# Six tiles' decay chain instead of two ahead of a scan, and the order of two copies on ScalarE

## What is computed

```python
# soft mixture: each token's row is a weighted mean of 8 x 128 processed slots
out = einsum('bnd,bsn->bsd', processed.reshape(b, e*t, d), softmax(logits.reshape(b, s, e*t)))
x = x + gb * out
# layer 1: modulated layer norm, then a second layer norm, then the projection W_in
h = layernorm(x) * (1 + ca) + sa
normed = layer_norm(h, gamma, beta)
dt = softplus(normed @ W_in[:, -8:] + b_in + dt_bias)      # one value a token and head
decay = exp(dt * A)                                        # 8 heads
h_t = decay_t * h_{t-1} + (dt_t * xs_t) B_t ; y_t = C_t h_t
```

## Time and profile before

| | |
|---|---|
| time, median of 3 runs | 1759.81 us (1759.13 to 1760.4) |
| the profiled execution | 1759.81 us, its span 1758.1 us |
| PE busy | 1642.9 us, 93% of the span |
| DVE busy | 1209.1 us, 69% |
| ACT busy | 732.0 us, 42% |
| POOL busy | 544.9 us, 31% |
| granted TensorE clock, mean | 0.98 |
| the combining loop of b = 1, with its tail | 845.3 to 931.2 us |

### The profile page before, as it was taken

How to read it: one execution, slowest core, us unless ns; L and a number is a source line. 1 busy time by engine, 2 the same in 40 slices (tenths; PEclk the granted TensorE clock), 3 DMA queues, 4 the chain that set the end, 5 groups by cost and what they waited for, 6 DMA issues and landing times. The chain is left out here.

```text
span 1758.1 us, 25512 instructions
## 1 busy us (share of the span) xinstructions
PE 1642.9 (93%) x9248; PEld 1383.2 (79%) x9248; DVE 1209.1 (69%) x2662; ACT 732.0 (42%) x1443; POOL 544.9 (31%) x446
## 2 busy tenths in 40 slices
PE   6999989989999999979987999999989999999996
PEld 4788878888867888856876888888768787888895
DVE  6877678764435655636686899999967845666663
ACT  3333333343324234424525666666621224444442
POOL 2100020000000003222252666666600023777764
PEclk9999999999999999989987999999999999999998
DMA  6000000010010000020116122232141123656553
GB/s 221 4 1 1 1 1 1 1 49 1 1 48 1 1 13 13 29 95 26 52 33 209 61 76 76 76 87 81 63 145 60 60 60 119 171 134 171 132 128 37
DMA packets 80248, 111.55 MB, mean 63 GB/s; under 512 B 15982, under 2 KB 60154, under 8 KB 79868
## 3 DMA queue, kind: packets, MB, share of 16 engines
q1 hardware_dynamic: 66172, 91.43, 16.1%
q0 software_dynamic: 12288, 17.31, 5.5%
q10 hardware_dynamic: 1664, 1.18, 0.2%
HBM read 81.59 MB, written 27.68 MB: 62 GB/s over the span
## 5 line engine op out<-in xcount | busy, mean ns | idle before, releaser
L2915 POOL DMA_INDIRECT out<-k_eo,idx x64 | 117.3, 1832 | 75.4 <-DVE k_eo L3007 60.7
L1816 POOL DMA_INDIRECT k_xe<-rows_dram,idx x64 | 82.5, 1289 | 178.8 <-DVE idx L2848 140.7
L1665 PE MATMUL d_pO<-d_sp,d_raw 128*128 128x257 f32 x512 | 116.6, 385 | 2.8 <-ACT d_raw L1460 2.7
L1665 PEld LDWEIGHTS d_pO<-d_sp,d_raw 128*128 128x128 f32 x512 | 96.9, 192 | 18.1 <-ACT d_raw L1460 3.5
L537 ACT ACTIVATE b_p<-b_pS,b_nmax 128x2048 f32<-128x2048 f32 (+14 forms) x32 | 40.6, 1270 | 141.2 <-DVE b_nmax L678 141.2
L61 PE MATMUL b_pO<-b_vh,b_ph 128*128 128x256 f32 x302 | 88.0, 291 | 4.4 <-DVE b_pl L660 4.3
L62 PE MATMUL b_pO<-b_vh,b_pl 128*128 128x256 f32 x302 | 85.7, 284 | 0.0
L63 PE MATMUL b_pO<-b_vl,b_ph 128*128 128x256 f32 x302 | 85.5, 283 | 0.0
L333 POOL TENSOR_TENSOR x<-x,b_vrow 128x256 f32<-128x256 f32 x32 | 24.0, 782 | 187.8 <-DVE b_hs L606 187.7
L2006 ACT ACTIVATE g_dlm<-g_cumb,g_cs 128x128 f32<-128x128 f32 x256 | 78.4, 393 | 2.5 <-DMA g_cumb<-cum_dram 2.5
L1441 ACT COPY d_raw<-d_pL 128x512 f32<-128x512 f32 x64 | 37.4, 588 | 93.4 <-PE d_pL L63 93.4
(11 more groups left out here) (568 smaller groups left out, 5336.8 us busy)
## 6 DMA issues: line engine op xcount, KB each, us to landing
g_cumb<-cum_dram SPq DMA_DIRECT2D x32, 512.0 KB, 4.2
k_wf<-in_WgT SPq DMA_DIRECT2D x16, 512.0 KB
k_wf<-in_WuT SPq DMA_DIRECT2D x16, 512.0 KB
k_wf<-in_WdT SPq DMA_DIRECT2D x16, 512.0 KB
rows_dram<-h_hx SPq DMA_DIRECT2D x32, 136.0 KB, 3.9
x<-in_x SPq DMA_DIRECT2D x8, 512.0 KB, 9.5
d_w<-in_w SPq DMA_DIRECT2D x4, 1024.0 KB, 6.2
uT_dram<-d_ug SPq DMA_DIRECT2D x16, 256.0 KB, 2.4
```

Of the source, the lines that this page charges most:

```text
L1665: last = nc.tensor.matmul(pO[:, t % 2, 0:PW], raw[e][:, t * P:(t + 1) * P], proc[e], start=e == 0, stop=e == E - 1)
L1816: nc.gpsimd.indirect_dma_start(out=m.xe[:, e % 2, t, :], out_offset=None, in_=m.rows, in_offset=bass.IndirectOffsetOnAxis(ap=column(m, e, ...
L2915: nc.gpsimd.indirect_dma_start(out=out, out_offset=bass.IndirectOffsetOnAxis(ap=column(m, e, t), axis=0), in_=eo[:, e % 2, t, :], in_offse ...
```

## The change

The second run of the decay chain takes six tiles of b = 1 instead of two (48 columns instead of 16), and the third, in the next stage, ten instead of 14 (80 columns instead of 112). Since its input is complete only with pair 2's step sizes, its parts stand later in the combining loop. Two more "dt" and one more "u" are moved from the tail into the loop, and the tail's order is changed. On ACT, `state_normed(q + 1)` is put ahead of `state_turned(q)` for every pair of b = 1.

```diff
-        late = [[("u", q) for q in range(PAIRS - 3) if 2 * q + 5 == t] + [("dt", q) for q in range(PAIRS - 4) if 2 * q + 6 == t] for t in range(NTB)]
-        tail = [("dt", PAIRS - 4)] + [(kind, q) for q in range(PAIRS - 3, PAIRS) for kind in ("u", "dt")]
+        late = [[("u", q) for q in range(PAIRS - 2) if 2 * q + 5 == t] + [("dt", q) for q in range(PAIRS - 2) if 2 * q + 6 == t] for t in range(NTB)]
+        tail = [("dt", PAIRS - 3), ("u", PAIRS - 2), ("u", PAIRS - 1), ("dt", PAIRS - 2), ("dt", PAIRS - 1)]
...
-                        if t in (0, 8):
-                            log_ratio(t // 8)
-                        if t in (1, 10):
-                            decay_sizes(t // 10)
-                        if t in (3, 13):
-                            keep_sums(t // 13)
-                        if t in (5, 15):
-                            keep_turned(t // 15)
+                        if t in (0, 11):
+                            log_ratio(t // 11)
+                        if t in (1, 13):
+                            decay_sizes(t // 13)
+                        if t in (3, 15):
+                            keep_sums(t // 15)
+                        if t == 5:
+                            keep_turned(0)
...
-            step_sizes(1, PAIRS - 4)
             state_rows(1, PAIRS - 1)
-            step_sizes(1, PAIRS - 3)
+            keep_turned(1)
             state_offset(1, PAIRS - 1)
-            for q in range(PAIRS - 2, PAIRS):
-                residual(q)
-                step_sizes(1, q)
+            for kind, q in tail:
+                if kind == "dt":
+                    if q >= PAIRS - 2:
+                        residual(q)
+                    step_sizes(1, q)
...
             for q in range(PAIRS):
-                state_turned(1, q)
                 if q + 1 < PAIRS:
                     state_normed(1, q + 1)
-                if q == 0:
+                state_turned(1, q)
+                if q == m.decayed // 2 - 1:
                     decay_exp(1)
-                if q == 1:
                     decay_log(1)
-                if q == 3:
+                if q == m.decayed // 2 + 1:
                     decay_sums(1)
...
-                        if t in (2, 10):
-                            cumulate(t // 10)
-                        if t in (4, 14):
-                            turn_sums(t // 14)
+                        if t in (2, 14):
+                            cumulate(t // 14)
+                        if t in (4, 15):
+                            turn_sums(t // 15)
...
-    m.decayed = 2
+    m.decayed = 6
```

## The result

The changed kernel takes 1770.42 us (median of 4 runs, 1768.61 to 1773.76) against 1759.47 for the kernel before beside it: 1.0063 times, 95% interval 1.0046 to 1.0081. It is slower, as forecast, but by 10.95 us instead of 4.5, and 2.1 us above the top of my range. The profiled execution took 1773.93 us, its span is 1772.2, at a mean granted clock of 0.975 against 0.98.

The account below looks back on a forecast made before the run. PE is busy 93% of the span, but DVE paces the combining loop (9.8 us a pair against 8.3). 1759.81 + 4.0 (chain through ACT) + 0.5 (tail) = 1764.3 us; range 1759.8 to 1768.3.

Parts of the forecast that it names:

- The chain on ACT: Combining loop: closed chain offset, norming, copy, "dt", step sizes, rows makes O(6), the time of DVE's `state_offset(6)`, 4.0 us later.
- odd work: DVE's extra work at odd t in the loop: `output_low` twice, 2.3 us, and the decay chain's small instructions, 2.4.
- The lock: Rival, chance 0.03: in the loop DVE and POOL lock SBUF ports per instruction, `state_rows` 4.7 instead of 4.06 us; 1767.5.
- Slow spells: Rival, chance 0.12: each PE wait in the loop brings a slow-clock spell, 3.2 us more, 1767.5 us.
- The tail: After `state_offset(7)`: DVE ends 0.9 us later, nothing if the DMA write of pair 7's copy sets the barrier; 0.5 counted.
- The next stage: Shorter decay chain there, gain counted as nothing because ACT waits for gate weights; 0.7 us the bound.
- That six tiles win nothing: Combining loop: PE's 3.87 us wait for dA and the slow combine behind it vanish, without gain, since DVE sets the pace.

Follow-up runs that it names:

- a1: Changed kernel with ACT's old order (copy of pair q ahead of norming of pair q + 1): 1764.32 us, ratio 1.001.
- c2: Changed kernel with ACT's old order and DVE's two `output_low` moved to t = 2 and 4: 1760.24 us, ratio 0.9992.
- c1: Kernel before with DVE's two `output_low` moved from t = 7 and 9 to t = 2 and 4: 1760.51 us, ratio 0.999.
- a3: Changed kernel with unread matmuls filling PE's waits ahead of each "dt" in the loop: 1768.9 us, and 1767.55 when run again.

## Why the prediction was right in direction and wrong in size

**The chain on ACT (forecast +4.0 to O(6)): right, a little high.** All that it names is in the profile: PE waits for the copy, DVE for "dt", no wait for dA. From an offset to the rows behind it I had 3.53 us; the pairs at the full clock show 3.51, 3.52 and 3.51 (for example O(2) at 885.06 and the rows at 888.57). The rows themselves were to take 4.06 and take 3.64 to 3.93. Without slow spells the five pairs cost 52.11 against the forecast 52.95: +3.2 instead of +4.0, of which the shorter turns give 0.7, since a turn without odd work is 10.53 less 1.14, 9.39, where I had 9.53.

**The lock (chance 0.03): refuted.** It asked 4.7 us for the rows; the longest is 3.93, with DVE's two shared instructions at 2.15. The Trainium skill's rule (SBUF — State Buffer, "SBUF: two separate sides") of an exclusive lock for a whole instruction isn't what these rows show: POOL's instruction takes 1.26 us while DVE waits and 1.26 to 1.44 beside DVE's rows.

**Slow spells (chance 0.12, +3.2): this is the step that failed.** I gave it a low chance because of one wait of 2.43 us that was followed by the full clock, and took the unknown stretch between 2.43 and 3.87 for the place where it would be decided. In the changed kernel the waits that bring a spell are 2.73, 2.00 and 1.90 us, in a1 one of 1.53 and one of 0.69 do, in c2 one of 1.94 does not, and the very wait of the earlier trace rows is followed by a granted clock of 0.50 to 0.57 over 2 us in six of the other 13 profiles. One row was no bound: the outcome isn't a function of the wait's length alone. Its price was too low as well, 3.2 against 5.0, although it counted a spell behind all five waits: two of the waits were 0.39 and 0.69 us instead of 2.0 to 2.7, since the slow combine before each had used them up, and the third spell cost nothing. The first was to cost 0.4 and cost 1.7, the last was to cost 1.7 and cost 3.2. I let a combine behind a wait end at O + 9.1; the first ends at about O + 10.3 (883.12 less 872.80), because "dt" itself runs slow (1.64 instead of 0.95) and the combine takes 6.45 and not 5.7; the last, with `cumulate(1)` inside the spell, ends at O(5) + 11.0 (927.94 less 916.90). The Trainium skill describes that pattern, a wait in each turn of a loop and a slow clock behind each (TensorE: Matmul & The Clock Gate, "HAM oscillation — how this bites in real kernels"); the page has it for longer waits, for a DMA, and the rows agree for three of five waits.

**The tail (+0.5 of 0 to 0.9): 0 was right.** DVE ends later, as worked out: its last `step_sizes` starts at O(7) + 6.4 (940.77 less 934.40) instead of 5.7. The barrier doesn't move: the next stage's first DVE instruction comes at O(7) + 8.50 (942.90), and before at O(7) + 8.59:

```profile
933.96 0.48 DVE L2099 MEMSET mod<- 128x512 f32 x1 [2.75 <-PEq L50]
```

DVE idles 1.96 us in front of it now and idled 2.75 before. It isn't DVE that opens the barrier. It is the write of pair 7's copy, as argued. The queue's last wait of the stage, in the kernel before:

```profile
SPq L1029 <- DMA uT_dram<-d_ug: 1.7, 1, 1.7
```

It ends at about 931.81 before and 940.75 after, 2.15 us ahead of DVE's memset both times, and as much ahead in eight other profiles, while the end of DVE's last instruction lies anywhere from 1.95 to 2.76 us ahead.

**The next stage (gain 0, bound 0.7): right.** Its first scan matmul comes 16.1 to 16.4 us after the memset in ten of the fourteen profiles, with 112 columns and with 80 (17.9 to 20.4 in the others, of both kinds), and ACT waits for the gate weights 6.59 us instead of 5.95:

```profile
961.83 0.23 ACT L2072 ACTIVATE h_mgw<-h_gw 128x32 f32<-128x32 f32 x1 [6.59 <-DMA h_gw<-in_gate_wT]
```

**That six tiles win nothing: right.** The wait of 3.87 us looked like the prize; a1 removes most of it and the loop is 0.3 us longer, since DVE is the bound. c1 shows it from the other side.

**The account.** The loop: 3.1 for the chain with its tail and 5.0 for the slow spells, 8.0 of the 10.95 us (unrounded 3.07 and 4.97). The sum with the right terms, 1759.8 + 8.0, is 1767.8, still 2.6 under the measurement. What makes up the rest **stays open**. The first profile has 3.4 us in the stretch behind the next stage's first scan matmul, the second none; the stage behind it shows 1.5 and 1.8 in both, but equal code shows up to 4.8 there in other kernels (37.6 to 42.4). Slow spells come and go all over this kernel from one execution to the next; over the executions of all kernels a mean granted clock lower by 0.001 goes with about 1.1 us, fitted with one slope and an offset for each kernel. At equal mean clock the changed kernel is 6.4 to 6.6 us above the kernel before, the filled one 4.9, a1 1.1 and c1 0.8 below. So more than the spells within the loop may be in it, and no experiment separated that.

## What to carry to other kernels

Before an instruction is put ahead of another on an in-order engine, follow what its releaser waits for: here the norming needed DVE, DVE needed "dt", and "dt" needed the copy that was pushed behind the norming, so that one swap closed a chain through three engines and set the pace of five turns. Then ask what else in the same change adds a place where this chain bites: the fifth "dt" that the new lists put into the loop cost nothing with the old order and 3.7 us with the new. A wait that vanishes wins nothing when the engine waited for is the bound; look at that engine's gaps first. And price every new wait of TensorE twice, with the full clock behind it and with half of it, unless rows of the same kernel show many such waits and not one.

## What was not expected of the hardware

Waits of 1.53 to 2.73 us, and one of 0.69, in a loop in which PE is otherwise busy were followed by some microseconds at 1.2 GHz: the combine behind took 5.40 to 6.45 us instead of 3.64. A wait of 1.94 us was not (3.72, c2), and neither was another of 0.69. Matmuls that nobody reads in place of the wait kept the full clock in both profiles (3.72). And the kernel before spreads over 1756.4 to 1770.4 us in its executions beside the experiments, so 2.8 us won in one stage (c1) can't be told from nothing, and a profiled execution can be 5 to 6 us off the median of its own kernel, as a3's was.
